# Four of the eight token groups of a feed-forward layer's second product computed by seven quarter products each

## What is computed

```python
next_h = jnp.tanh(xw_t + prev_h @ Wh)             # recurrence
h = jax.nn.relu(quant_linear(x, w1, b1))          # first product, D -> F
y = quant_linear(h, w2, b2)                       # second product, F -> D
x = x + y
# quant_linear: x to 0..255 by one scale, w to int8 by one scale per row, b to its product's steps
```

## Time and profile before

| | us |
|---|---|
| median of three runs | 486.65 (486.13 to 487.23) |
| the profiled execution's own time | 487.11 |
| its span, first to last instruction | 485.2 |
| PE busy | 474.3 (98%) |
| DVE busy | 300.5 (62%) |
| ACT busy | 235.5 (49%) |
| POOL busy | 94.8 (20%) |

### The profile page before, as it was taken

One profiled execution on the slowest core, in us unless ns is written; L12 is line 12 of the kernel. 1 busy time (PEld: TensorE's weight loads), 2 busy tenths in 40 slices (PEclk: granted clock), 3 DMA queues, 4 the chain that ended last, 5 costly groups with the idle time before them and its releaser, 6 DMA issues.

```text
span 485.2 us, 8663 instructions
## 1 busy us (share of the span) xinstructions
PE 474.3 (98%) x3000; PEld 324.7 (67%) x3000; DVE 300.5 (62%) x491; ACT 235.5 (49%) x452; POOL 94.8 (20%) x69
## 2 busy tenths in 40 slices
PE   8999999999999999999899999999999999999996
PEld 3688888888999999999865444444443444444442
DVE  2789956358454454544678899878777443344442
ACT  0326554454233332322588788888865333343330
POOL 2833290400000000000000000000002355544345
PEclk9999999999999999999999999999999999999999
DMA  8974522200449000000000276700002388888882
GB/s 293 387 280 165 183 88 86 88 1 1 86 87 173 0 1 0 0 0 0 2 1 0 101 319 288 325 13 0 0 0 88 104 307 309 316 292 288 303 307 110
DMA packets 38168, 65.41 MB, mean 135 GB/s; under 512 B 19056, under 2 KB 19200, under 8 KB 34560
## 3 DMA queue, kind: packets, MB, share of 16 engines
q1 hardware_dynamic: 37472, 64.04, 38.3%
q10 hardware_dynamic: 576, 1.05, 0.6%
q0 software_dynamic: 96, 0.01, 0.0%
HBM read 39.93 MB, written 20.97 MB: 126 GB/s over the span
## 4 chain that ended last, share of the span: by engine, by line
PE 93%; DVE 3%; ACT 1%; DMA 1%; issue 1%; DVEq 0%; ACTq 0%
PE bank L958 22%; PE bank L823 21%; PE bank L620 18%; PE bank L657 12%; PE bank L663 12%; PE bank L647 3%; PE bank L705 3%; PE bank L683 1%; DMA arena<-x_t 1%; ACT arena L1157 1%; DVE slot_max L1510 1%; DVE arena L1504 0%; ACT arena L1163 0%; DVE late_max L1731 0%; ACT bank L1150 0%
## 5 line engine op out<-in xcount | busy, mean ns | idle before, releaser
L596 POOL TENSOR_SCALAR arena<-arena,bq 128x512 f32<-128x512 f32 x32 | 54.0, 1702 | 328.0 <-DVEq L1806 276.4
L823 PE MATMUL bank<-arena,w_words 128*128 128x512 f16 (+1 forms) x512 | 112.5, 379 | 0.4 <-issue 0.4
L958 PE MATMUL bank<-arena,w2t 128*128 128x512 f16 x512 | 110.7, 379 | 0.5 <-DVE arena L1769 0.5
L1163 ACT ACTIVATE arena<-bank,bq,s_bits 128x512 f32<-128x512 f32 (+1 forms) x126 | 90.1, 766 | 21.8 <-PE bank L823 16.1
L958 PEld LDWEIGHTS bank<-arena,w2t 128*128 128x128 f16 x512 | 49.7, 98 | 61.5 <-DVE arena L1763 2.0
L823 PEld LDWEIGHTS bank<-arena,w_words 128*128 128x128 f16 x512 | 49.5, 98 | 58.5 <-issue 0.9
L1722 DVE TENSOR_REDUCE hid_parts<-arena 128x1 f32<-128x1024 f32 x60 | 70.7, 1216 | 13.0 <-ACT arena L1163 12.7
L657 PE MATMUL bank<-arena 128*128 x512 | 63.5, 277 | 0.0
L663 PE MATMUL bank<-arena 128*128 x512 | 62.4, 275 | 0.0
L657 PEld LDWEIGHTS bank<-arena 128*128 128x128 f32 x512 | 59.7, 192 | 0.6 <-issue 0.4
L663 PEld LDWEIGHTS bank<-arena 128*128 128x128 f32 x512 | 59.7, 192 | 0.0
(11 more groups left out here) (110 smaller groups left out, 359.9 us busy)
## 6 DMA issues: line engine op xcount, KB each, us to landing
spill<-arena SPq DMA_DIRECT2D x12, 1024.0 KB, 3.9
arena<-spill SPq DMA_DIRECT2D x12, 1024.0 KB, 8.1
arena<-w SPq DMA_DIRECT2D x8, 1024.0 KB, 5.1
arena<-x_t SPq DMA_DIRECT2D x32, 256.0 KB, 3.8
y_t<-arena SPq DMA_DIRECT2D x32, 256.0 KB, 2.1
arena<-x_t SPq DMA_DIRECT2D x7, 1024.0 KB, 8.8
arena<-x_t ACTq DMA_DIRECT2D x4, 256.0 KB, 5.6
arena<-wx SPq DMA_DIRECT2D x4, 256.0 KB, 5.4
```

What stands on the lines that cost most here:

```text
L596: nc.gpsimd.tensor_scalar(xb[:, d], xb[:, d], bq2[:, d:d + 1], None, ALU.add).then_inc(xb_ready, 1)
L823: return nc.tensor.matmul(bank[:, at, :], w1t[:, k, f * P:(f + 1) * P], states_in[:, k, :], start=(k == 0), stop=(k == KT - 1))
L958: return nc.tensor.matmul(bank[:, 4 + d, :], w2t[:, f, d * P:(d + 1) * P], hq[:, f % HQ_RING, :], start=(f == 0), stop=(f == FT - 1))
L1163: return nc.scalar.activation(out[:, cols], bank[:, at, cols], ACT.Identity, bias=bq1[:, f:f + 1], scale=s1_bits[:, f:f + 1])
```

## The change

The groups are taken in the order 4, 3, 0, 5, 1, 6, 2, 7 (ORDER; the place in it is n). The groups at n = 0, 1, 3, 5 are computed as before (PLAIN). Those at n = 2, 4, 6, 7 (groups 0, 1, 2 and 7; BY_QUARTERS) are computed as a 2 x 2 by 2 x 2 block product in the scheme of Strassen and Winograd: tiles halved in the hidden index (c) and the output index (r), tokens halved (t), seven products of quarter size, each of 16 matmuls of 256 columns.

- ACT makes all eight pairs of such a group in place in its slot (whole_pairs), group 7 in slot 0 after its fetch. DVE makes four sums of quarters (f16, 128 x 2048), for group 7 in halves between its other work, and four sums of the weights once, in the space of w1.
- Three banks collect the products. DVE takes each product out of its bank into xb with two operations of 128 x 256 (take), seven times per group; PE waits for takes before it adds on.
- xb is doubled. SP's list is per n: four stores, four loads for n + 2, and fetches of quarters k (0 to 3 of group 5, 4 to 7 of group 6, 8 to 11 of group 7) as in the table fetches.
- The loops over the groups are written out; keep_going reads w2t.

```diff
+ORDER = (LAST, 3, 0, 5, 1, 6, 2, 7)
+BY_QUARTERS = (2, 4, 6, 7)
+PLAIN = (0, 1, 3, 5)
+HALF_F = FT // 2
+QUARTER_BANKS = ((0, 1, 2), (0, 1, 2), (0, 1, 2), (4, 5, 6))
+FROM_SPILL_AT = 0
+TAKEN = 5
...
+        xb_pair = [part(at, KT * GTOK).rearrange("p (k t) -> p k t", k=KT)
+                   for at in (last_tiles * GTOK, 0)]
+
+        def xb(n):
+            return xb_pair[n % 2]
+
+        quarter_words = keep_words // QUARTERS
+        assert KT * GTOK == quarter_words and last_tiles * GTOK == 3 * quarter_words
+        places = ([quarter_words, 2 * quarter_words]
+                  + [keep_at + 3 * keep_words + n * quarter_words for n in range(QUARTERS)]
+                  + [quarter_words, 2 * quarter_words]
+                  + [keep_at + FROM_SPILL_AT * keep_words + n * quarter_words
+                     for n in range(QUARTERS)])
...
+        def w2_sum(m):
+            area = w1_words[:, m * w2_words:(m + 1) * w2_words].bitcast(F16)
+            return area.rearrange("p (f n) -> p f n", f=HALF_F)
...
-            def fetch(s, quarters):
-
-                sp.wait_ge(relu_ready, (s + 1) * (PAIRS - len(OWN)))
...
-                    sp.wait_ge(spilled[n], 16 * SPILL)
-                    if s > 0:
-                        sp.wait_ge(fetched[n], 16 * s)
-                    at = PLACE[SPILLED[s]] * keep_words + n * piece
-                    nc.sync.dma_start(keep_flat[:, at:at + piece],
-                                      spill[s, :, n * piece:(n + 1) * piece]).then_inc(fetched[n], 16)
-
...
+            def fetch(k):
+                s, n = k // QUARTERS, k % QUARTERS
...
+                    sp.wait_ge(own_ready, 3 * len(OWN))
+                else:
+                    sp.wait_ge(quarter_made, 7)
+                sp.wait_ge(spilled[n], 16 * SPILL)
+                if s > 0:
+                    sp.wait_ge(fetched[n], 16 * s)
+                nc.sync.dma_start(part(places[k], quarter_words),
+                                  spill[s, :, n * piece:(n + 1) * piece]).then_inc(fetched[n], 16)
...
+            def load_again(n):
 
...
-                    sp.wait_ge(y_stored[d], g * 16)
-                    nc.sync.dma_start(xb[:, d], xTk_v[tokens(g), d]).then_inc(xb_landed[d], 16)
+                    if n > 1:
+                        sp.wait_ge(y_stored[d], (n - 1) * 16)
+                    nc.sync.dma_start(xb(n)[:, d], xTk_v[tokens(ORDER[n]), d]).then_inc(xb_landed[n % 2][d], 16)
...
-            for g in range(2 * SPILL):
-                store(g)
-                load_again(g + 1)
-                fetch(g // 2, (0, 1) if g % 2 == 0 else (2, 3))
-            store(GROUPS - 2)
-            load_again(GROUPS - 1)
-            store(GROUPS - 1)
+            load_again(0)
+
+            sp.wait_ge(relu_ready, 1)
+            sp.wait_ge(own_ready, 1)
+            load_again(1)
+            fetches = {0: (0, 1), 1: (2, 3, 4), 2: (5, 8, 9), 3: (6, 7, 10), 4: (11,)}
+            for n in range(GROUPS):
+                if n == 0:
+                    for k in fetches[0]:
+                        fetch(k)
+                store(n)
+                if n + 2 < GROUPS:
+                    load_again(n + 2)
+                for k in fetches.get(n, ()) if n > 0 else ():
+                    fetch(k)
...
-                            pe.wait_ge(y_ready, g * KT + d + 1)
+                            if g > 0:
+                                pe.wait_ge(y_ready, Y_RING + PLAIN[g - 1] * KT + d + 1)
...
-            with pe.Fori(0, GROUPS) as g:
-                second_products(g)
+            def quarter_product(at, weights, hidden_quarter, first=False):
+                for f in range(HALF_F):
+                    for j in range(2):
+                        mm = nc.tensor.matmul(bank[:, at, j * HALF:(j + 1) * HALF],
+                                              weights[:, f, j * P:(j + 1) * P], hidden_quarter[:, f, :],
+                                              start=(first and f == 0 and j == 0),
+                                              stop=(f == HALF_F - 1), skip_group_check=True)
+                mm.then_inc(quarter_made, 1)
+
+            def products_by_quarters(i):
+                g = ORDER[BY_QUARTERS[i]]
+                chain_bank, plain_bank, other_bank = QUARTER_BANKS[i]
+                pe.wait_ge(whole_made, (i + 1) * PAIRS)
+                if i > 0:
+
+                    free_after = max(n for n in PLAIN if n < BY_QUARTERS[i]) if i == 3 else (
+                        BY_QUARTERS[i - 1])
+                    pe.wait_ge(y_ready, Y_RING + (free_after + 1) * KT)
+                quarter_product(chain_bank, w2_part(0, 0), whole_part(g, 0, 0), first=True)
+                quarter_product(plain_bank, w2_part(1, 0), whole_part(g, 1, 0), first=True)
+                pe.wait_ge(w2_sums, 2)
+                pe.wait_ge(whole_sums, 4 * i + 3)
+                pe.wait_ge(quarter_taken, TAKEN * i + 1)
+                quarter_product(chain_bank, w2_sum(1), whole_sum(g, 2))
+                quarter_product(other_bank, w2_sum(0), whole_sum(g, 1), first=True)
+                pe.wait_ge(w2_sums, 4)
+                pe.wait_ge(quarter_taken, TAKEN * i + 3)
+                quarter_product(chain_bank, w2_sum(2), whole_sum(g, 3))
+                pe.wait_ge(quarter_taken, TAKEN * i + 4)
+                quarter_product(other_bank, w2_sum(3), whole_part(g, 1, 1))
+                pe.wait_ge(whole_sums, 4 * i + 4)
+                pe.wait_ge(quarter_taken, TAKEN * i + 5)
+                quarter_product(chain_bank, w2_part(1, 1), whole_sum(g, 4))
+
+            for n in range(GROUPS):
+                if n in BY_QUARTERS:
+                    products_by_quarters(BY_QUARTERS.index(n))
+                else:
+                    second_products(PLAIN.index(n))
...
+            def whole_pairs(i, first, end):
+
+                g = ORDER[BY_QUARTERS[i]]
+                for pair in range(first, end):
+                    if pair > 0:
+                        act.wait_ge(whole_made, i * PAIRS + pair)
+                    if g in SPILLED:
+                        act.wait_ge(fetched[2 * pair // QUARTERS], (SPILLED.index(g) + 1) * 16)
+                    nc.scalar.activation(whole_ints(g, pair),
+                                         keep[:, whole_slot(g), 2 * pair:2 * pair + 2, :],
+                                         ACT.Relu, scale=s_hid_inv[:, 0:1]).then_inc(whole_made, 1)
...
+            def scale_output(i):
...
-            relus(0, lambda f: keep[:, 0, f:f + 2, :], first=True)
+            ring_pair(0, 2)
+            ring_pair(0, 6)
+            whole_pairs(0, 0, 2)
             act.wait_ge(scales2_ready, 1)
-            with act.Fori(1, LAST) as g:
-                relus(g, lambda f: keep[:, g, f:f + 2, :])
-            relus(LAST, None)
-            with act.Fori(SPILLED[0], GROUPS) as g:
-                relus(g, lambda f: keep[:, g - SPILLED[0], f:f + 2, :],
-                      fetches=g - (SPILLED[0] - 1))
+            ring_pair(0, 10)
+            whole_pairs(0, 2, 4)
+            ring_pair(0, 14)
+            whole_pairs(0, 4, 6)
+            ring_pair(1, 2)
+            scale_output(0)
+            ring_pair(1, 6)
+            whole_pairs(0, 6, 8)
+            ring_pair(1, 10)
+            ring_pair(1, 14)
+            for i in range(2):
+                ring_pair(i + 2, 2)
+                scale_output(i + 1)
+                ring_pair(i + 2, 6)
+                whole_pairs(i + 1, 0, PAIRS)
+                if i == 1:
+                    whole_pairs(3, 0, PAIRS // 2)
+                ring_pair(i + 2, 10)
+                ring_pair(i + 2, 14)
+            whole_pairs(3, PAIRS // 2, PAIRS)
+            scale_output(3)
...
+            def w2_sum_made(m, a, b, op):
+                if m in (1, 3):
+                    dve.wait_ge(w2_sums, m)
+                nc.vector.tensor_tensor(w2_sum(m), a, b, op).then_inc(w2_sums, 1)
...
+            def first_sums(i):
+
+                g = ORDER[BY_QUARTERS[i]]
+                dve.wait_ge(whole_made, (i + 1) * PAIRS)
+                difference(g, 1, whole_part(g, 0, 1), whole_part(g, 0, 0))
+                difference(g, 3, whole_part(g, 1, 1), whole_part(g, 0, 1))
+
+            def second_sums(i):
+
+                g = ORDER[BY_QUARTERS[i]]
+                dve.wait_ge(whole_sums, 4 * i + 1)
+                difference(g, 2, whole_part(g, 1, 1), whole_sum(g, 1))
+                dve.wait_ge(whole_sums, 4 * i + 3)
+                difference(g, 4, whole_part(g, 1, 0), whole_sum(g, 2))
+
+            def take(i, made, r, t, at, done):
+
+                n = BY_QUARTERS[i]
+                dve.wait_ge(quarter_made, 7 * i + made)
+                if made > 1:
+                    dve.wait_ge(quarter_taken, TAKEN * i + min(made - 1, TAKEN))
+                for j in range(2):
+                    d = 2 * r + j
+                    dve.wait_ge(xb_ready, n * KT + d + 1)
+                    block = xb(n)[:, d, t * HALF:(t + 1) * HALF]
```

(133 more changed lines are left out.)

117 lines of the change are left out of this document (57 added, 60 removed).

## The result

The kernel after takes **498.75 us** (median of four runs, 498.36 to 499.06); the kernel before took 486.44 beside it. The ratio is 1.025 (95% interval 1.0232 to 1.0268): 12 us slower, where 481.8 was forecast. The profiled execution took 498.99 us, its span 497.2.

A forecast was written before the change was run, and what follows sets the result against it. PE's product work was taken to bound the last stage, with DVE, ACT and the DMA queue hidden. Products -6.4, tail -0.3 and fetch wait +1.8 gave -4.9, so 481.8 us after the median correction; range 479.8 to 487.9.

The forecast's parts named there:

- PE: Last stage's products: 112 matmuls of 256 columns at 0.109 us make a quarter group 12.2 us, not 13.82; -6.4 over four.
- DVE: Takes at 0.48 us and f16 sums at 1.2 in the last stage, hidden behind PE's products: cost 0.
- the rival by the port: DVE's sums and POOL's operations block each other on SBUF, each sum waiting 1.56 us: 486 to 487; within a 0.07 chance.
- Tail: From the last product to the last output: two takes, 1.0 us against 1.27 before, so -0.3.
- SP and the queue: SP's stores, loads and fetches through one queue: last fetch k=11 lands at t 80.1, PE loses 1.8 us.
- k=11 lands at 35.3 + 16 m: Landing of the last fetch, behind 16 transfers of 1.05 MB in an always busy queue: 80.1 with 2.8 per transfer.
- m: Microseconds per 1.05 MB transfer in the DMA queue: 2.8 taken, between ends of 2.71 and 3.3.
- t: Time in us from the last stage's first product, forecast at 370.11.
- The deadline: k=11 must land by t 78.3 for PE's third quarter product at n = 6; any later landing is PE's loss.
- The rival on the other side: k=11 lands after t 85, at 88.1; PE idles 9.8 us in the group at n = 6: 489.8, chance 0.13.
- DVE falling behind: If f16 sums cost 2.26 us, takes come late and PE loses 6 us: 486, chance 0.07.
- dearer matmuls: A 256-column matmul costs more than 0.109 us in the quarter products; break-even 0.123, chance 0.04.

The follow-up runs named there:

- e1: The changed kernel without the twelve transfers from spill; SP only raises the semaphores, so groups 5 to 7 are computed from what lies in the slots: 479.20 us.
- e5: The changed kernel with e2's early fetch list and a semaphore of its own for each of the twelve fetches: 480.01 us.
- e6: The changed kernel with its own SP list, only with a semaphore for each fetch: 492.31 us.
- e11: e6 with fetches k=2 to 5 moved ahead of the stores of the group at n = 1, the rest of the list as in the change: 488.90 us.
- e2: The changed kernel with SP's list alone changed: k=2 to 5 ahead of the stores at n = 1, the other six ahead of those at n = 3: 483.29 us.
- e8: The changed kernel with 48 idle products put into PE's wait in the group at n = 6: 495.94 us.
- e9: The changed kernel with ACT making the scaling before the last two pairs of group 7; DVE's first half sum waits for six pairs, not four: 487.16 us.
- e7: The changed kernel with all twelve fetches issued by ACT on its own queue with own semaphores, SP keeping stores and loads alone: 489.94 us.
- e4: The changed kernel with three groups by quarters instead of four (group 7 plain) and e2's list: 484.55 us.
- e3: The changed kernel with three groups by quarters instead of four (group 7 plain), SP's list as in the change: 488.04 us.
- e10: The changed kernel with three groups by quarters instead of four (group 7 plain) and e5's list and semaphores: 482.23 us.

## Why the prediction was wrong

**PE: right.** The whole stage without waits is 104.36 us in e1 and e5, against 104.2. The quarter products space at 0.109 (sixteen in 1.91 with 0.273 for one), the value taken.

**DVE: right.** From the kernel after, the takes' row among the groups by line, and the row of the sums alone (ns min/median/max, first to last start):

```profile
L1954 DVE SCALAR_TENSOR_TENSOR arena<-bank,s_bits,arena 128x256 f32<-128x256 f32 x56 | 24.5, 479 | 16.3 <-PE bank L1074 16.1
L1927 DVE TENSOR_TENSOR arena<-arena x12: 1218/1220/1631, 390.1 to 450.5; 128x2048 f16<-128x2048 f16 x12
```

Takes 0.479 (0.48 taken), sums 1.220 (1.2 taken). The Trainium skill, VectorE: DVE Perf Modes, in the perf-mode table, gave 1.22 for the latter; the trace agrees. The worst sum beside POOL took 1.63, so the rival by the port, a whole wait of 1.56 per sum, didn't happen on DVE. POOL paid more: beside the four sums of order 2 (390.13 to 395.66) one of its operations took 3.42 instead of 1.56. Four sums and two of those operations ran side by side in 5.5 us; at 1.22 and 1.56 each they are 4.9 and 3.1 apart (spans on POOL are rough), so they slowed each other without shutting each other out. PE never waited for a sum.

**Tail: right.** From the end of the last product to the end of the last take it is 0.92 us (493.47 to 494.39), where 1.0 was forecast against 1.27 before. The kernels without a wait gained 6.4 (e5) and 7.2 (e1); -6.7 was the sum of products and tail.

**SP and the queue: the step that failed.** The forecast wrote "k=11 lands at 35.3 + 16 m" "with work always waiting" and took m = 2.8. k=11 landed at 465.2, t 95.0, which makes m = (95.0 - 35.3) / 16 = 3.73, outside all bounds. The step that failed is "with work always waiting": the formula was fed with rates of transfers, and the time went to transfers that SP hadn't issued yet. Three things held them back. First, the wait for an earlier fetch's landing, in the diff in plain sight (`if s > 0`): 6.4 us by e6. Second, the place of the fetches: they stand behind loads, which wait for the landing of stores, which lie in the queue behind earlier fetches. I wrote that chain down and then counted bytes only. Third, the queue idle from 391 to 397, before the stores of order 1. e11 took the third away (3.4 us more), and e5 the second (another 8.9). These shares go by the order of the steps: with the early list in place, the semaphores were worth 3.3 (e2 against e5). A queue that was full did reach 2.8 (e5, 379 GB/s over 21 us), and for 10 us 417 GB/s. The Trainium skill, DMA: Bandwidth & Descriptors, has 425 GB/s for 16 MB from one core in its section Bandwidth, which agrees with that far better than the 358 of its Specifications that I weighed.

**The deadline: right, but only half used.** The formula gives 95.0 - 78.3 = 16.7 us lost in order 6. 11.4 came of it, since 3.4 + 1.7 had already been lost in order 5 and moved the deadline back. That earlier wait, for k=6, I hadn't priced at all: I gave k=11 a deadline and no other fetch. Every fetch has one. PE ran dry at 443.07, k=6 landed at 445.65, and one pair of DVE's (0.75) stood between landing and product.

**The clock: missed.** A wait of PE was priced at its length. Here the stretch at the lower clock behind each cost 1.7 and 2.4 us more; e8 shows it for the 2.4. The two together are 4.1 of the 18.9.

**The rival on the other side** had the right mechanism and chain, "slower: k=11 comes after t 85", with 0.13 and 489.8. In kind it is what happened, but it hung on the same m, so its size was 9 us short. DVE falling behind and dearer matmuls are out by e1 and e5.

## What to carry to other kernels

Price an issuing queue by its list, not by its bytes: write issue and landing time of each transfer, with each wait of the issuer, and compare every landing with its own reader's need. Ask of each wait in such a list whether it protects data or is only a shared semaphore; twelve semaphores and an earlier place for the fetches turned +12 us into -6.4. And where an engine's list puts work that may be late ahead of work that the critical engine needs now, swap them: beside the late fetches that was worth 11.6 us (e9).

## What the runs showed of the hardware beyond that

- A queue filled with six fetches makes each land later (up to 16.5 us after issue in e5 against 12.0 in the change, the stores behind them after 14.9) and the last of them sooner, at 437.7 instead of 465.2.
- SP's and ACT's queue share one rate: 422 GB/s together (e7), 417 for one alone (e5). The Trainium skill, DMA: Bandwidth & Descriptors, Queues, rings and completion order, has both as rings of the same 16 engines; the trace agrees.
- Every wait of PE of 2.0 us or more was followed by a stretch at the lower clock, and what that cost didn't grow with the wait. By the matmuls behind it: 1.7 us behind waits of 2.0 (e2), 3.7 (e4) and 3.2 (the change), 1.7 and 1.6 behind 2.3 and 2.5 (e9), 2.9 behind 4.2 (e3), 2.6 behind 5.3 (e11), 1.5 behind 8.2 (e7), 1.6 behind 9.5 (e6) and 2.4 behind 11.2 (the change). Waits of 0.6 us (e6), 0.9 (e8) and 1.75 (e10) cost nothing more: 7.08 for 32 matmuls and 7.15 for 64 behind them. Why the price differs is open.
- Most kernels whose PE waited scatter over 2.7 to 6.4 us (the widest is e9), those without a wait (e1, e5) over 1.0 to 1.1. The change itself, with two long waits, scattered over 0.7, and e8 over 1.3; why is open.
